# Two residual blocks on one core: the first feed-forward's squares on DVE instead of POOL, with new orders and banks

## The reference

```python
def _L0_ffn_ref(x, fast_b, w_fc, w_proj, u, v, gate):
    ...
    h = _bitlinear(x, w_fc) + gate * (x @ v.T @ fast_b.T @ u.T)
    r = jnp.maximum(h, 0.0)
    return _bitlinear(r * r, w_proj)
...
x = L0_attn_x
x = x + _layernorm(_L0_attn_ref(_layernorm(x, axis=-1), ...), axis=-1)
x = x + _layernorm(_L0_ffn_ref(_layernorm(x, axis=-1), ...), axis=-1)
x = x + _layernorm(_L1_attn_ref(_layernorm(x, axis=-1), ...), axis=-1)
x = x + _layernorm(_L1_ffn_ref(_layernorm(x, axis=-1), ...), axis=-1)
```

## Time and profile before

| what | value |
|---|---|
| median of three runs | 1388.17 us (1387.15 to 1388.91) |
| the profiled execution's own time | 1383.91 us |
| its span, first to last instruction | 1382.1 us |
| busy: PE, DVE, ACT, POOL | 1194.7, 1103.5, 1054.4, 346.8 us |
| mean granted TensorE clock | 0.946 of full speed |
| squares on POOL (line 784) | 64 instructions, 83.6 us |
| rectifications on ScalarE (line 1235) | 64 instructions, 42.7 us |

### The profile page before, as it was taken

The page is one execution under the profiler, slowest core; times in us unless marked ns, Lnnn a source line. Parts: engine busy times, 40 slices in busy tenths (PEclk is TensorE's granted clock), DMA queues, the critical chain, the costliest instruction groups (busy, mean ns, idle before and its releaser), DMA issues.

```text
span 1382.1 us, 23204 instructions
## 1 busy us (share of the span) xinstructions
PE 1194.7 (86%) x8060; PEld 775.0 (56%) x8060; DVE 1103.5 (80%) x2259; ACT 1054.4 (76%) x2111; POOL 346.8 (25%) x317
## 2 busy tenths in 40 slices
PE   4788995889899989899899999999999998782867
PEld 2575663466556755566656765675655765451434
DVE  2694278999688888989798998899799988988930
ACT  4575699868967998699967989698959887547532
POOL 2953202520133203221134101530133101401021
PEclk9799997999999999999999999999999999896879
DMA  7511341315133104512334131613252131013000
GB/s 235 123 25 36 85 132 41 101 37 140 47 77 90 34 19 145 123 31 54 111 78 98 24 110 39 145 24 96 69 105 57 24 125 31 30 51 105 16 16 16
DMA packets 72084, 101.65 MB, mean 74 GB/s; under 512 B 10640, under 2 KB 44064, under 8 KB 71968
## 3 DMA queue, kind: packets, MB, share of 16 engines
q1 hardware_dynamic: 71968, 100.16, 27.7%
HBM read 74.44 MB, written 25.69 MB: 72 GB/s over the span
## 4 chain that ended last, share of the span: by engine, by line
PE 37%; ACT 23%; DVE 22%; issue 9%; POOL 5%; DMA 2%; SPq 1%; DVEq 0%; POOLq 0%; ACTq 0%
PE ps L885 12%; PE ps L894 10%; DVE work L1526 7%; PE ps L968 4%; ACT work L1213 4%; ACT xnd L1156 3%; DVE work L1449 3%; PE ps L986 3%; ACT work L1220 3%; PE ps L1053 2%; PE ps L960 2%; DVE work L1517 2%; ACT work L1280 2%; POOL later_norms L764 2%; DVE work L1535 2%
## 5 line engine op out<-in xcount | busy, mean ns | idle before, releaser
L1526 DVE TENSOR_TENSOR_SCAN work<-work 128x512 f32<-128x512 f32 x256 | 318.5, 1278 | 38.5 <-ACT work L1280 35.7
L1213 ACT ACTIVATE work<-work 128x384 f32<-128x384 f32 (+3 forms) x512 | 266.4, 564 | 46.0 <-DVE work L1449 45.1
L764 POOL TENSOR_TENSOR later_norms<-later_norms,singles 128x2 f32<-128x2 f32 x112 | 100.8, 903 | 689.4 <-ACT xnd L1156 387.0
L1449 DVE CUSTOM_DVE_ANT_0 work<-ps,work 128x384 f32<-128x384 f32 (+3 forms) x512 | 223.6, 484 | 49.7 <-PE ps L960 47.3
L968 PE MATMUL ps<-ident,work 128*128 128x128 f32 x1280 | 198.9, 280 | 26.8 <-ACT work L1213 21.1
L968 PEld LDWEIGHTS ps<-ident,work 128*128 128x128 f32 x1280 | 149.7, 144 | 76.9 <-issue 51.2
L1220 ACT COPY work<-ps 128x512 f32<-128x512 f32 x300 | 172.0, 580 | 0.4 <-PE ps L968 0.2
L1535 DVE TENSOR_TENSOR work<-work 128x1024 f32<-128x1024 f32 x128 | 162.4, 1269 | 5.1 <-DVEq L1373 0.2
L960 PE MATMUL ps<-work 96*128 96x384 bf16 (+3 forms) x512 | 123.1, 307 | 10.9 <-DMA work<-scratch 8.3
L894 PE MATMUL ps<-wpr,hid 128*128 128x256 f32 x512 | 119.7, 393 | 10.4 <-POOL hid L784 10.4
L894 PE MATMUL ps<-wf,hid 128*128 128x256 f32 x512 | 119.3, 395 | 4.4 <-ACT hid L1296 3.6
(11 more groups left out here) (177 smaller groups left out, 1934.9 us busy)
## 6 DMA issues: line engine op xcount, KB each, us to landing
work<-values SPq DMA_DIRECT2D x64, 256.0 KB, 3.5
work<-ratios SPq DMA_DIRECT2D x64, 256.0 KB, 3.1
scratch<-work SPq DMA_DIRECT2D x32, 384.0 KB, 4.7
work<-scratch SPq DMA_DIRECT2D x64, 192.0 KB, 3.9
work<-scratch SPq DMA_DIRECT2D x64, 128.0 KB, 4.2
x_in<-x SPq DMA_DIRECT2D x8, 512.0 KB, 7.0
work<-scratch SPq DMA_DIRECT2D x64, 64.0 KB, 4.4
values<-work SPq DMA_DIRECT2D x16, 256.0 KB, 2.4
```

The source lines that it names most:

```text
L764: g_.tensor_tensor(rstds[chain][:, tokens], spreads[chain][:, tokens], power[:, tokens], ALU.pow).then_inc(*rstd.one)
L1213: i = s_.activation(part_of, part_of, ACT.Exp, scale=-1.0, bias=nmax[:, row:row + 1])
L1449: i = v_.tensor_tensor_reduce(sc[:, n % 4, at:at + nk], out_of(b, name)[:, at:at + nk], base_of(qt), -SCORE_SCALE, BIG, ALU.add, ALU.min, ...
L1526: v_.tensor_tensor_scan(ring[:, at, m, :], pwr[:, slot, :], ring[:, at, m, :], 0.0, ALU.mult, ALU.add).then_inc(*scanned.one)
```

## The change

The squares move from POOL to DVE. For item `fc` n, ScalarE rectifies the bank into `hid[:, n, :]` as before and counts a semaphore `hid_cut`, and no longer drains the bank. DVE waits for that count and multiplies the rectified rows in SBUF by the rows that still stand in PSUM: where a row is negative the rectified one is zero, so the product is the square of the rectified row. DVE's product drains the bank, and `fproj` waits for the drains of `fc6` and `fc7`. POOL loses the item, DVE gets it, and all orders (`MERGE`) and all banks (`BANKS`) are new, so items stand in other places on all five engines, in the preparation too.

```diff
     "pe": ...
-        "a2 p a4 p a3 p2 a p a p a27 p a3 p a4 p a26 p a p a11 p2 a13 p a p a7 p a19 d a2 d2 a4 d6 a3 d a9 d a2 "
+        "a10 p2 a4 p4 a34 p a11 p a31 p5 a6 p a7 p2 a20 d a2 d9 a8 d a8 d a7 d a3 d2 a18 d a2 d2 a3 d3 a13 d2 a d "
...
 BANKS = """
-0123450123450132450132450132401534025430243502435124035241324512435214302154321042310234120345201342
+0123450123450134250134250134201532045203420532045120345201420512405214032154021342103421042315420314
...
-    "dve": "stats ckv q qr k kr base S T OT sum fsum z weights ratio total rates turn frac scan mix gate silu "
+    "dve": "stats ckv q qr k kr base S T OT sum fc fsum z weights ratio total rates turn frac scan mix gate silu "
...
-    "pool": "stats q k ystats fstats fc fystats zstats oystats gstats gystats gsum ternary tables late",
+    "pool": "stats q k ystats fstats fystats zstats oystats gstats gystats gsum ternary tables late",
...
-        hid_sq = signal("hid_sq", HC)
+        hid_cut = signal("hid_cut", HC)
...
-                if item == "fc":
-                    is_drained(pool, b, f"fc{n}")
-                    g_.tensor_tensor(hid[:, n, :], hid[:, n, :], hid[:, n, :], ALU.mult).then_inc(*hid_sq.one)
...
                 if item == "fproj":
-                    need(pe, hid_sq, b, HC)
+                    is_drained(pe, b, "fc6")
+                    is_drained(pe, b, "fc7")
                     token_out(b, "fproj", n, hid, wpr, HC)
...
                 if item == "fc":
                     is_filled(act, b, f"fc{n}")
-                    s_.activation(hid[:, n, :], out_of(b, f"fc{n}"), ACT.Relu, bias=zero[:, 0:1]
-                                  ).then_inc(*drains(b, f"fc{n}"))
+                    s_.activation(hid[:, n, :], out_of(b, f"fc{n}"), ACT.Relu, bias=zero[:, 0:1]).then_inc(*hid_cut.one)
...
+                if item == "fc":
+                    name = f"fc{n}"
+                    need(dve, hid_cut, b, n + 1)
+                    v_.tensor_tensor(hid[:, n, :], out_of(b, name), hid[:, n, :], ALU.mult).then_inc(*drains(b, name))
```

More of the change, by code:

```diff
@@ L174 @@
     "pe":
[10 rows of a table removed]
-    "act":
[15 rows of a table removed]
-    "dve":
[12 rows of a table removed]
[9 rows of a table added]
+    "act":
[14 rows of a table added]
+    "dve":
[13 rows of a table added]
     "pool":
-        "a p a4 p4 a4 d2 a3 d15 a4 d2 a3 d16 a7 d18 a d2 a d a2 d a3 d18 a d4 a5 d a d17 a d4 a3 d2 a3 d20 a7 d22 "
-        "a2 d34 p4",
+        "a2 p a3 p4 a4 d2 a3 d7 a4 d2 a3 d8 a4 d2 a3 d8 a d3 a d a5 d10 a d4 a6 d10 a d4 a3 d2 a3 d9 a d3 a6 d14 "
+        "a2 d26 p4",
     "sp":
-        "a13 d2 a m4 d3 m13 a7 d3 m2 d m6 d m5 a3 m a2 m2 d m d a2 d3 m4 d m d m8 a3 m a2 m3 d2 a2 d2 m4 d2 m4 d "
-        "m5 a m a4 m3 d2 a2 d2 m4 d2 m6 d m5 a3 m a2 d m d a2 d4 m8 d m5 a2 m a3 m2 d m d a2 d2 m4 d2 m5 d m7 d m "
-        "d4 m4 d2 m13 d4",
+        "a14 d3 m4 d m4 d m9 a6 d2 a m4 d3 m10 a5 m d m2 d a2 d3 m4 d2 m9 a5 m2 d m2 d a2 d3 m4 d m4 d m5 a3 m a2 "
+        "m3 d2 a2 d2 m4 d2 m2 d m9 a3 m a2 m d2 a2 d3 m4 d m5 d m5 a5 m2 d m d a2 d3 m4 d m4 d m8 d m d3 m4 d3 "
+        "m13 d4",
@@ L221 @@
 }
 BANKS = """
-0123450123450132450132450132401534025430243502435124035241324512435214302154321042310234120345201342
-0352430152431502674315607423516074235160742310546372051364253041625301764520376512750261754206152765
-4306153143405413025140365241064735106423514206351435120647351206437512064315042675140263542310643201
-3674103675146021546270516742503614570321673417023672146210356274130754137217267672054371620543715204
-3715204372470163457123406752346503742653071243061753672601536123065241653425145342731532417365402164
@@ L230 @@
-5106754106237514062713450627467146702134567213456712345076123457103625413240652134025617306134270534
-6754203752340715243712540672471562047512463720134572630517263405172065341720653406517240651740625173
-4506241735604723105742130752341065302176375401741645067541602576405170165307165326017365412763570256
-4710265473210546731246053124312640531264035712640532714562703146724036743126034571632470562752740652
-4602653746507314620436710432760134520714635016257306241536213651730462517304516270541267054167253014
@@ L235 @@
-6725036210735612075316450312476052465740237064372160327106316034516304125364207641205436105736412057
-612340576123057612430576123457623104576210453762104537621045
+0123450123450134250134250134201532045203420532045120345201420512405214032154021342103421042315420314
+2354123054120534671205637142056371402563714056743510762450162405176425703142671450621547621057426017
+2305473243640762304672534076237154623705467023546705462371054623710546237045263056412354576213576157
+2301672530713207163021376012473560417326570243560376423526013754206514051735352646540217635402137540
@@ new lines @@
+1375240137524631574326743640176035476314605237416507124501762507142063547260143617304613740156723641
+3057613054762130547630215476305274163052741630542163054635321403765410642504136205436104275316471256
+4157261750623716520753012752073157235163720561326372406137024561374537025370621475036217241750267502
+4130567412564273015231706253716231540716520462745206742657014271064214710245172035470157263140652316
+7346521730517462305167240516705162405716240573425321067451046145304261534605421730652714637256473256
@@ L237 @@
+4357042364507560276250763125703624135067215473507214536074574261305742613507261350267350216340572163
+4507123013675210372607514306712546170256172065137305216372130710235170423150726140375624705647123056
+413702564137256413072564132056432170564317052643170526431705
 """
```

## The result

The changed kernel takes 1364.87 us in the median (1361.44 to 1369.83); the ratio to the kernel before is 0.985 with the interval 0.9829 to 0.987, so 21 us faster (0.015 x 1387.66; 1387.66 us is the median of the kernel before in the same comparison). A second measurement gave 0.9838 (0.9824 to 0.9853). The second measurement left a second profile of the change, of 1361.90 us; against it the trace of before shows 22.0 us.

What follows compares the result with a forecast made beforehand. No engine alone was the bound: TensorE, ScalarE and DVE hand it to each other. Terms -5.0 - 2.0 + 3.9 + 0.6 = -2.5 us on the 1388.17 us median gave 1385.7 us, range 1372 to 1401.

Steps and rivals of the forecast that it cites:

- The rest of the orders and banks: All engines' new item orders and banks, same work per engine: taken as 0, with 8 us allowed either way.
- Batches 2 to 6, +3.9 us: Middle batches: 40 products, 27.6 us, less 10 us of stretching, give DVE 17.6 us more, counted at 22%: +3.9 us.
- rival 1: DVE's queue late at `fproj` in batches 2 to 6, 2.6 us five times: +13 there, 1394.8 us; chance 0.25.
- Rival 2: The middle's 10 us of stretching all on the chain, products all in idle time: -16.4, 1371.8 us; chance 0.20.
- sign for a change of over 14 us: Whole kernel: a change over 14 us either way would say the new orders, not the squares, set the result.
- Batch 7, -5.0 us: `fold` moved behind the eighth rectification on ScalarE, so `fproj` starts 5.0 us earlier: -5.0 us, ends -5.7 and 0.
- rival 3: DVE's 6.0 us idle after batch 7's `fproj` does not shrink, the -5.0 is lost: +2.5, 1390.7 us; chance 0.10.
- Batch 1, -2.0 us: Four POOL squares in a row leave the chain; unstretched DVE work pays for eight products: -2.0 us, ends -2.2 and 0.
- PSUM, 0 us: `fc` banks freed by the product, at least 0.69 us later, 64 times; TensorE's bank waits 0.2 us before: taken as 0.
- The product isn't stretched: DVE's products, one SBUF input, take no lock: 0.69 us each; if stretched, at most 21 us more in batches 1 to 7.
- DVE's busy time: Sign that the forecast is right: DVE's busy time over the run up by about 44 - 22 = 22 us.
- ScalarE, +0.6 us: 43 table loads in place of 41, 2.6 us, at ScalarE's 23% of the chain: +0.6 us, ends 0 and 2.6.

Runs made afterwards that it cites:

- experiments 2, 3 and 4: Kernel before, squares on POOL, with: DVE's first two items swapped (0.9985); batch 7's last fold behind eighth rectification (0.9987); new orders up to 150 us (0.9997).

## Why the prediction was wrong

The forecast was -2.5 us, the measured change -21, outside the range of -16 to +13.

*The step that failed* is "The rest of the orders and banks is new everywhere ... I allow a seventh of it, 8 us, either way, and take 0". From the old orders with products to the change it is 0.985 against 1.0026, -24 us. The table by stretch shows where (old orders with products, against the two profiles of the change). From batch 1's first scan to batch 6's it is -15 and -17 us; the 8 us were a share of TensorE's idle time just there. Before batch 0's first scan it is -8 and -9, in a stretch of which the prediction read one window. In batch 1 it is +5, and behind batch 6's first scan -4 and -8, in all -22 and -30 in these traces. The step's deeper fault is that it took the orders as a term of their own. Orders found with the product in DVE's queue decide what the product costs: 25 us in the old, 4 to 6 in the new.

*Batches 2 to 6, +3.9 us,* was the second. Its sizes hold: the four mixer operations are 23.1 us over their medians in the middle before and 13.8 in the old orders without squares, so the squares' part is 9.3 where the prediction took 10. Its weight of 22% was used for both halves. For the stretching the traces don't refute it: from batch 1's first scan to batch 6's, squares on POOL cost the old orders 1.1 us by the trace of before and 4 to 6 by three others with the same order there (766.8 to 768.7 in the runs of experiments 2, 3 and 4 that have it), where 22% gave 2.2. For the products it fails both ways: they cost 12.4 us in the old orders, 45% of their 27.6, and -0.1 and 2.2 in the new, by the two profiles. Against before, products in the old orders make +11.3 us, where rival 1 had +13, but not by rival 1's wait: from the last `fc` to `fproj` the five batches take 1.0 us more than before in all (19.5 against 18.5), not 2.6 us each. The change makes -3.8 and -6.1, where the forecast had +3.9.

Rival 2 came nearest in the sum, 1371.8 us, with a chance of 0.20. The part that has the products in idle time holds for the middle of the new orders. The part that has 10 us of stretching there on the chain is not shown: it is 1 to 6 us in the old orders and 5.5 in the new (763.4 against 757.9). And 7 to 8 us of the gain come before batch 0's first scan, of which this rival said nothing. That it came so near is in part luck. What the runs do bear out is that the stretching is paid for: with all of POOL's work and no wait for it, the kernel is as slow as before, and the whole run's 20.8 us of DVE (1103.5 - 1082.7, the prediction's 22) went with 21 us of time, by these traces more than half of it in batches 1 and 7.

The prediction's own sign for a change of over 14 us, that the new orders and not the squares set the result, is half right. The orders alone give 14.8 us, but leaving the squares out of the old orders gives 21.

*Batch 7, -5.0 us.* At its own place it came as worked out: the wait fell by 5.6 us, products took 0.69 us, `frac` 747 ns and `turn` 478 in that stretch. The prediction had no term for TensorE's clock, and it added to the gain: the second product took 14.05 us at 1.00 in place of 16.79 at 0.84. From the end of the eighth `fc` to the first scan it is 49.3 us (48.9 in the second profile) where it was 55.9. But the cut of the chain alone, in the old orders, is worth 1.8 us with POOL and nothing with DVE. That is rival 3's mechanism: DVE holds the end. With the whole new tail it is 6 to 8 us, by a run that has a seam of its own.

*Batch 1, -2.0 us.* In the old orders from the first scan of batch 0 to that of batch 1 it is 150.7 against 153.1 us, -2.4. Without squares it is 146.8, so the four squares on the chain cost 6.3 us, and the products 3.9 in their place. There the term was right. In the change the same stretch is 155.7 us, 2.6 longer than before, so the gain of this batch did not come with the new orders.

*PSUM, 0 us.* The banks did become scarcer: 4.7 us of waits where the earlier trace rows have 0.2. Taking 3.7 of them away gave nothing clear of the noise, so the value stands as far as can be told, and its reason (no wait) doesn't. The rule of the Trainium skill's page "PSUM — Partial Sum Buffer" ("Summary: rules for kernel authors"), to empty PSUM promptly, shows in this wait and not in the time.

*The product isn't stretched:* 659 to 693 ns in all 64. This agrees with the Trainium skill's page "SBUF — State Buffer" ("SBUF: two separate sides"), by which a DVE instruction with one SBUF input, outside the two-port modes, takes no lock; that DVE's SBUF-to-SBUF work lost 20.8 us to POOL's squares agrees with it too.

*DVE's busy time* rose by 11.1 us, not 22: products add 35 to 37 us (1118.1 - 1082.7 in the old orders, 1114.6 - 1077.3 in the new), not 44. In part that is overlap: behind 53 of the 64 the next instruction starts some 0.08 us before the product has ended. And DVE's other work is 5 us less in the new orders than in the old (1082.7 and 1077.3 without squares), as the mixer's operations there are 5 us less over their medians in the whole run (16.1 and 10.7).

*ScalarE, +0.6 us,* was not tested apart.

What stays open: which pieces of the new orders in the middle batches are worth what (a cut there leaves a seam, and one run with a seam was 28 us worse), how the 6 us that they gain without squares divide between the start and the tail, and how much of any of these prices is TensorE's clock.

## What to carry to other kernels

Price a stretched instruction apart from an added one, and place by place: in these old orders more than half of the stretching was paid for in batches 1 and 7 and half of the added products in the long middle, and one share of the chain did not fit both. Where a change brings new orders, compare the orders from their first item on, before any share of idle time is allowed for them; one early item that waits for a load held up the whole start here. To tell whether an engine's work costs by its lateness or by its running, let it run and let nobody wait for it. Look at the granted clock of a stretch, and at a second profile of the same kernel, before a difference is put down to one cause.

## What was not expected of the hardware

POOL's 64 squares of 128x512 cost DVE 20.8 us, 0.33 us each, and with their results unused the kernel was as slow as with them (1.0008): taking the wait for them away gave nothing. Leaving them out gave 21 us, so over the whole run DVE's loss and the kernel's are about the same, though DVE had 22% of the chain. And the second product of batch 7 took 14.05 to 14.08 us at a granted clock of 1.00 where TensorE had stood idle for 0.78 or 1.55 us before it, but 16.28 and 16.79 us at 0.86 and 0.84 where it had stood idle for 5.13 or 7.19.
